# Token-major values, key blocks of 64 and two-turn attending in a six-layer local-attention kernel

## The chip, the cores and the metric

The kernel runs on one core of a Trainium2 chip. The metric is the device time of one execution in microseconds (us); less is better. TensorE is called PE here, ScalarE ACT, VectorE DVE, GpSimd POOL and the queue that issues the DMAs SP.

## The reference, cut to what matters

The input is 4 sequences of 512 tokens with 128 features. A global causal attention with 16 heads comes first; neither its code nor its work is changed. Then six layers follow, each a local attention and a gated feed-forward part. What the change touches is the local attention of every layer:

```
def attn_layer(x, Wqkv, qs, ksc, Wo):
    q, k, v = split(shift_tokens(x) @ Wqkv)          # 16 heads of 64 features
    q, k = rotary(l2norm(q) * qs), rotary(l2norm(k) * ksc)
    sim = einsum(q, k of this window of 32 and the one before) * 8
    sim = where(query < key or query > key + 32, -max, sim)
    return (softmax(sim) @ v) @ Wo
x = attn_layer(...) + x;  x = ffn_layer(shift_tokens(x), ...) + x
```

## The kernel before

The layers are a software pipeline written out by hand, one program for each engine, with a semaphore for each hand-over. A body is one layer of one sequence (24 bodies); it has two halves, `a = 0` and `a = 1`, each with 4 pairs of heads. There are 48 halves `n`. While half `n` is attended, the queries, keys and values of half `n + 1` are projected, and the feed-forward parts of earlier bodies are put in between (`v0`, `v1`, `v2`, `down`, `wo0`, `wo1` in a first half; `mean`, `var`, `g0`, `g1`, `g2` in a second one). PE's program for the middle 20 bodies is a loop of two bodies run 10 times; the other engines' programs are unrolled.

PE does the following in a half, in this order: `project` 0 and `value_tile` 0; `max_scores` in two parts, with `project` 1 and `value_tile` 1 around them; `norm2(0)`, `turn_max`; `project` 2; `turned_scores` for the even key windows, `value_tile` 2, `turned_scores` for the odd ones; `project` 3; `value_tile` 3; `norm2(1)`; `sum_probs`; `attend_local` for even windows, a feed-forward step, `attend_local` for odd windows.

- `project(i)` makes queries and keys of one pair of heads: each of the two is three passes of 512 columns over operands that POOL has split into a high and a low part (`three`, fp32r, one instruction each).
- `value_tile(t)` makes values of 128 tokens: 16 products of 32 tokens by 128 columns in plain fp32, put on the four column groups of PE, so that 32 keys of each pair lie on their own 32 partitions. A plain fp32 matmul shows as two in the trace, each with a weight load of its own.
- `turned_scores(e)` puts mask and row maximum into a bank with 2 bf16 products and adds 64 fp32 products of 32 keys by 64 queries; ACT takes the exponent of 1024 columns (`exps`).
- `sum_probs` sums over keys (8 products of 256 columns), ACT turns the sums to inverses by Ln and Exp (`invert_sums`, 256 columns), and SP stores and spreads them by DMA for POOL (`scale_out`).
- `attend_local(e)` adds 64 fp32 products of 32 keys by 64 queries.

One PSUM bank (`N_BANK`) serves the value tiles, the norms, the turned maxima and the sums in turn. `ring[0]` takes the projections, `ring[1]` and `ring[2]` the scores and what is attended. ACT empties banks in the order written in its own `body`: squares, `value_out`, `rnorm` (Ln and Exp of the norms), `max_rows`, `exps`, `invert_sums`. DVE rotates (`rope`) and multiplies by the spread norms (`final`), after which `max_scores` may start.

Of the kernel before, what the change touches and what calls it, by code (L numbers as in the profile page):

```python
# [7 lines left out]
F32 = mybir.dt.float32  # L8
# [26 lines left out]
BLOCKS = TOK // WINDOW  # L35
# [37 lines left out]
def shape_constants():  # L73
# [9 lines left out]
    token = np.arange(TOK)[None, :]  # L83
    own = np.arange(WINDOW)[:, None]
    by_key = np.zeros((P, TOK))
    for e in range(2):
        ahead = (token - WINDOW * e) % (2 * WINDOW) - own
        by_key[WINDOW * e:WINDOW * (e + 1)] = np.where((ahead >= 0) & (ahead <= WINDOW) & (token >= WINDOW * e),
                                                       0.0, MASKED)
    pick = np.zeros((P, 2, 2, P))  # L90
    for e in range(2):
        for h in range(2):
            for k in range(WINDOW):
                pick[WINDOW * e + k, e, h, k::WINDOW] = 1.0
            for pair in range(GROUP):
                pick[MAX_ROWS + 4 * (pair // 2) + 2 * h + pair % 2, e, h, WINDOW * pair:WINDOW * (pair + 1)] = 1.0
# [9 lines left out]
    in_pair = (part[:, None] // SLOT == col // (SLOT // GROUP)).astype(np.float32)  # L106
    squares = np.concatenate([eye, mean, in_head, in_pair], 1)
# [24 lines left out]
def build_program(nc, x, w_kqv, m, w_qkv, q_scale, k_scale, w_o, ln_g, ln_b, w_1, b_1, w_2, b_2,  # L132
                  rotary, masks, blocks, wide, out):
    with ExitStack() as ctx:
# [3 lines left out]
        def sem(name):  # L138
# [6 lines left out]
        MASKS = 2 * P + P + TOK + 4 * P  # L145
# [3 lines left out]
        warm16 = key_rows = mask_sb[:, 3 * P:3 * P + TOK]  # L149
        pick = [[mask_sb[0:MAX_ROWS + 8, 3 * P + TOK + (2 * e + h) * P:3 * P + TOK + (2 * e + h + 1) * P]  # L150
                 for h in range(2)] for e in range(2)]
        SQUARES = 2 * P + 2 * SLOT
        wide_sb = sb("wide_sb", [P, SQUARES + 2 * TOK + 12])
        eye, mean_w = (wide_sb[:, i * P:(i + 1) * P] for i in range(2))
        in_head, in_pair = (wide_sb[:, 2 * P + i * SLOT:2 * P + (i + 1) * SLOT] for i in range(2))
# [17 lines left out]
        w_hi = sb("w_hi", [P, 2, PAIRS, P], F32R)  # L173
        w_lo = sb("w_lo", [P, 2, PAIRS, P], F32R)
        wv_sb = sb("wv_sb", [P, PAIRS, P])
        w_raw = sb("w_raw", [P, 2, 2, P])
# [7 lines left out]
        x_shift = x_flat[:, 0:2 * TOK].rearrange("p (a t) -> p a t", a=2)  # L184
# [3 lines left out]
        raw = [sin_raw[:], x_flat[:, 2 * TOK:4 * TOK].rearrange("p (a t) -> p a t", a=2)]  # L188
# [198 lines left out]
        def queries(j, e):  # L387
            return min(2 * WINDOW, TOK - WINDOW * j)
# [5 lines left out]
        def _(sp):  # L394
# [68 lines left out]
            def store_inverses(n, a):  # L463
                sp.wait_ge(s_inv, n + 1)
                if some(n - 1):
                    sp.wait_ge(s_ib, 32 * (n - 1))
# [1181 lines left out]
```

## Time and profile before

| what | value |
|---|---|
| median of 3 runs | 2734.62 us (2728.51 to 2758.71) |
| profiled execution | 2722.72 us, its span 2720.9 us, 1.8 us around it |
| granted PE clock, mean | 0.872 |
| PE busy | 2033.8 us (75%), 44592 matmuls |
| PE weight loads busy | 1186.3 us (44%) |
| DVE, ACT, POOL busy | 1122.1, 1022.6, 949.9 us |
| chain that ended last | PE 61%, issue 14%, DVE 13%, ACT 8% |

### The profile page before, as it was taken

How to read it: one execution, taken by the hardware profiler on the slowest of the kernel's cores; microseconds unless marked ns; L12 is line 12 of the kernel's file. 1: busy time of each engine (PE TensorE's matmuls, PEld its weight loads, DVE VectorE, ACT ScalarE, POOL GpSimd, SP SyncE). 2: the span in 40 equal slices, each digit the busy share in tenths (PEclk: the TensorE clock that was granted, in tenths of full speed). 3: DMA queues.
4: the chain of work that ended last, by engine and by line, in shares of the span. 5: the costliest groups of instructions: out<-in, count | busy, mean ns of one | idle time of the engine just before them, and what ended most of it. 6: DMA issues, size and time to landing. Idle time of an engine off the chain costs nothing.

```text
span 2720.9 us, 96484 instructions
## 1 busy us (share of the span) xinstructions
PE 2033.8 (75%) x44592; PEld 1186.3 (44%) x44592; DVE 1122.1 (41%) x1198; ACT 1022.6 (38%) x1377; POOL 949.9 (35%) x621
## 2 busy tenths in 40 slices
PE   2999956777776777777778777777767777777875
PEld 1444434444444444444444444444444444444542
DVE  3444523354444434443433434344344344444441
ACT  1444423343333334333333433343333343344332
POOL 4222213233532434433344433235324244333320
PEclk9887768889898988899788799799889888899997
DMA  3000024454544544445445345444445444444441
GB/s 106 2 2 1 2 77 119 118 145 116 137 126 123 145 117 127 123 118 131 131 111 137 103 127 133 123 121 133 112 127 146 106 125 128 122 120 130 122 105 47
DMA packets 134834, 295.44 MB, mean 109 GB/s; under 512 B 23060, under 2 KB 48018, under 8 KB 127250
## 3 DMA queue, kind: packets, MB, share of 16 engines
q1 hardware_dynamic: 134418, 289.00, 39.6%
q8 instruction: 369, 6.05, 1.0%
q14 instruction: 47, 0.39, 0.0%
HBM read 177.54 MB, written 4.46 MB: 67 GB/s over the span
## 4 chain that ended last, share of the span: by engine, by line
PE 61%; issue 14%; DVE 13%; ACT 8%; DMA 1%; POOL 1%; SPq 1%; ACTq 0%; DVEq 0%; POOLq 0%
PE bank L996 6%; PE ring L979 5%; PE ring L694 5%; PE ring L952 5%; PE bank L901 4%; PE ring L696 4%; DVE rot L1507 4%; PE bank L877 4%; PE ring L695 4%; DVE rot L1500 3%; ACT sq L1218 3%; PE bank L1027 3%; ACT r_norm L1224 2%; PE bank L798 2%; PE ring L912 2%
## 5 line engine op out<-in xcount | busy, mean ns | idle before, releaser
L598 POOL TENSOR_TENSOR rot<-rot,t_sin 128x1024 f32<-128x1024 f32 x192 | 461.8, 2405 | 1306.8 <-DMA t_sin<-sin_raw 1306.8
L1496 DVE TENSOR_TENSOR sin_raw<-ring,tab_sb 128x1024 f32<-128x1024 f32 x192 | 235.1, 1225 | 1055.4 <-ACT sq L1218 995.7
L1218 ACT ACTIVATE sq<-ring 128x1024 f32<-128x1024 f32 x192 | 196.7, 1025 | 622.5 <-PE ring L696 622.5
L901 PE MATMUL bank<-wv_sb,x_tok 128*32 128x128 f32 x6144 | 236.9, 293 | 41.8 <-issue 41.6
L605 POOL TENSOR_TENSOR o_feat<-o_feat,inv_all 128x1024 f32<-128x1024 f32 x96 | 226.1, 2377 | 33.5 <-DMA inv_all<-inv_rows 33.5
L694 PE MATMUL ring<-xs_parts,w_hi 128*128 128x512 f32 x384 | 201.1, 524 | 45.3 <-issue 28.9
L1500 DVE TENSOR_TENSOR rot<-ring,tab_sb 128x1024 f32<-128x1024 f32 x192 | 233.2, 1215 | 0.0
L1507 DVE SCALAR_TENSOR_TENSOR rot<-r_all,rot 128x2048 f32<-128x2048 f32 x96 | 219.2, 2283 | 28.1 <-DMA r_all<-r_rows 27.8
L901 PEld LDWEIGHTS bank<-wv_sb,x_tok 128*32 128x32 f32 x6144 | 170.8, 116 | 123.0 <-issue 116.4
L1233 ACT ACTIVATE v_sb<-bank 128x512 f32<-128x512 f32 x192 | 114.8, 598 | 287.3 <-PE bank L901 287.1
L696 PE MATMUL ring<-xs_parts,w_lo 128*128 128x512 f32 x384 | 182.4, 475 | 44.3 <-issue 44.2
L979 PE MATMUL ring<-probs,v_sb 32*64 32x64 f32 (+1 forms) x12288 | 169.5, 236 | 54.0 <-issue 54.0
L979 PEld LDWEIGHTS ring<-probs,v_sb 32*64 32x64 f32 x12288 | 152.3, 135 | 104.6 <-issue 103.9
L1290 ACT ACTIVATE o_feat<-ring 128x1024 f32<-128x1024 f32 x96 | 97.9, 1022 | 217.5 <-PE ring L979 217.5
L695 PE MATMUL ring<-xs_parts,w_hi 128*128 128x512 f32 x384 | 179.3, 467 | 0.0
L996 PE MATMUL bank<-o_feat,wo_sb 128*128 128x512 f32 x384 | 174.9, 598 | 0.9 <-DVE state L1558 0.9
L952 PE MATMUL ring<-rot 64*32 64x64 f32 (+1 forms) x12288 | 153.2, 224 | 28.2 <-issue 27.8
L912 PE MATMUL ring<-mask_sb 128*128 128x512 bf16 x192 | 78.5, 501 | 126.3 <-DVE rot L1507 126.3
L952 PEld LDWEIGHTS ring<-rot 64*32 64x32 f32 x12288 | 133.7, 105 | 77.5 <-issue 77.4
L1430 DVE TENSOR_REDUCE inv_all<-ring 128x2 f32<-128x256 f32 (+3 forms) x128 | 104.0, 823 | 149.0 <-PE ring L758 148.3
L877 PE MATMUL bank<-sq,wide_sb 128*32 128x512 f32 x768 | 110.4, 646 | 49.5 <-ACT v_sb L1233 49.5
L694 PE MATMUL bank<-y_parts,w_hi 128*128 128x512 f32 x144 | 78.3, 543 | 87.3 <-DVE gates L1551 46.6
(147 smaller groups left out, 2918.2 us busy)
## 6 DMA issues: line engine op xcount, KB each, us to landing
t_sin<-sin_raw SPq DMA_DIRECT2D x384, 256.0 KB
r_all<-r_rows SPq DMA_DIRECT2D x192, 512.0 KB
inv_all<-inv_rows SPq DMA_DIRECT2D x96, 512.0 KB, 6.4
tab_sb<-in_rotary SPq DMA_DIRECT2D x6, 1024.0 KB
w_raw<-in_L_ffn_Wqkv SPq DMA_DIRECT2D x48, 128.0 KB, 3.4
wv_sb<-in_L_ffn_Wqkv SPq DMA_DIRECT2D x12, 256.0 KB, 6.7
wo_sb<-in_L_ffn_Wo SPq DMA_DIRECT2D x6, 512.0 KB, 8.9
x_tok<-state SPq DMA_DIRECT2D x24, 128.0 KB, 6.5
```

Of the source, the lines that this page charges most:

```text
L598: pool.tensor_tensor(dst, dst, t_sin[:], ALU.add).then_inc(s_rot, 1)
L694: pe.matmul(dst, lh, rh, start=True, stop=False)
L695: pe.matmul(dst, lh, rl, start=False, stop=False)
L696: return pe.matmul(dst, ll, rh, start=False, stop=True)
L901: mm = pe.matmul(N_BANK[SLOT * pair:SLOT * (pair + 1), j * P:(j + 1) * P], x_shift[:, par, at:at + WINDOW], wv_sb[:, 4 * a + pair, :], sta ...
L952: mm = pe.matmul(dst[SLOT * pair:SLOT * (pair + 1), h, at:at + wide_], rot[rows, a, pair, 1, at:at + WINDOW], rot[rows, a, pair, 0, at:at ...
L979: mm = pe.matmul(bank[2 + pair][DIM_HEAD * h:DIM_HEAD * (h + 1), at:at + wide_], v_sb[keys, a, col:col + DIM_HEAD], probs[keys, e, h, at:a ...
L996: mm = pe.matmul(F_BANK[:], wo_sb[:, a, :], o_feat[:, a, :], start=(a == 0), stop=(a == PAIRS - 1), skip_group_check=True)
L1218: act.activation(sq[:, i % 2, :, :], ring[0][:], ACT.Square).then_inc(s_sq, 1)
L1496: dve.tensor_tensor(sin_raw[:].rearrange("p a t -> p (a t)"), both, tab_sb[:, at + 2 * TOK:at + 4 * TOK], ALU.mult).then_inc(s_sin, 1)
L1500: dve.tensor_tensor(rot[:, a, i, :, :].rearrange("p a t -> p (a t)"), both, tab_sb[:, at:at + 2 * TOK], ALU.mult).then_inc(s_cos, 1)
L1507: dve.scalar_tensor_tensor(out=dst, in0=r_all[:], scalar=NORM_CAP, in1=dst, op0=ALU.min, op1=ALU.mult).then_inc(s_fin, 1)
```

## The change

Work is regrouped in the local attention of every layer; every result stays the same.

1. Values: `value_tile` is now `three` with the tokens as stationary operand: 3 fp32r passes of 512 columns in place of 32 matmuls. So the value weights have to be split too: `w_raw` loads three parts of a pair, and POOL's `split_pair` has 6 operations instead of 4. `wv_sb` and its loads go.
2. Keys lie in blocks of 64 with 96 queries each (4 strips of two blocks). `turned_scores(u)` makes all keys of two pairs of heads instead of half the keys of four. It uses `ring[1]` and `ring[2]` in both turns, so the second turn waits for both exponents of the first.
3. `sum_probs(u)` and `invert_sums(u)` run once for each turn, with 512 columns.
4. `attend_local(turn)`: 32 products of 64 keys by 96 queries each turn. The second turn adds to what the first wrote; PE waits for its own semaphore `s_at` between them.
5. `max_rows` is three copies instead of one. `x_shift` has one buffer instead of two.
6. SP stores inverses twice in a half.

```
-                for j in range(4):
-                    for pair in range(GROUP):
-                        at = WINDOW * (4 * t + j)
-                        mm = pe.matmul(N_BANK[SLOT * pair:SLOT * (pair + 1), j * P:(j + 1) * P],
-                                       x_shift[:, par, at:at + WINDOW], wv_sb[:, 4 * a + pair, :], start=True, stop=True)
-                mm.then_inc(s_v, 1)
+                rows = slice(t * P, (t + 1) * P)
+                three(N_BANK[:], (xs_parts[:, 2 * par, rows], xs_parts[:, 2 * par + 1, rows]),
+                      (w_hi[:, 2, 4 * a:4 * a + 4, :], w_lo[:, 2, 4 * a:4 * a + 4, :])).then_inc(s_v, 1)
...
+                    if some(n):
+                        pe.wait_ge(s_lns, 2 * n - 1)
...
+            def turned_scores(n, a, u):
+                if u == 0:
                     pe.wait_ge(s_nm, n + 1)
+                else:
+                    pe.wait_ge(s_e, 4 * n + 2)
+                for pair in range(2):
+                    dst = ring[1 + pair]
+                    for h in range(2):
+                        pe.matmul(dst[:, h, 0:STRIPS * SPAN], pick[4 * u + 2 * h + pair], key_rows[0:MAX_END, :],
+                                  start=True, stop=False, skip_group_check=True)
+                    for k in range(STRIPS):
+                        for c in range(2):
+                            at = KEYS * (2 * k + c)
+                            wide_ = queries(2 * k + c)
+                            for h in range(2):
+                                rows = slice(DIM_HEAD * h, DIM_HEAD * (h + 1))
+                                mm = pe.matmul(dst[KEYS * c:KEYS * (c + 1), h, SPAN * k:SPAN * k + wide_],
+                                               rot[rows, a, 2 * u + pair, 1, at:at + KEYS],
+                                               rot[rows, a, 2 * u + pair, 0, at:at + wide_],
+                                               start=False, stop=(k == STRIPS - 1), skip_group_check=True)
+                    mm.then_inc(s_st, 1)
...
+                strips = probs[:, u, :, :].rearrange("p i (k s) -> p i k s", s=SPAN)
+                for i in range(GROUP):
+                    dst = N_BANK[SLOT * i:SLOT * (i + 1), :].rearrange("p (k s) -> p k s", s=P)
+                    pe.matmul(dst[:, :, 0:SPAN], in_low, strips[:, i, :, :], start=True, stop=False,
+                              skip_group_check=True)
...
+            def attend_local(n, a, turn):
+                for u in range(2):
+                    for k in range(STRIPS):
+                        for c in range(2):
+                            pair = c if turn == 0 else 1 - c
...
@@ PE's body
                     turned_scores(n, a, 1)
+                    sum_probs(n, 0, end)
                     if not end:
                         project(gn, an, parn, 3)
...
-                    sum_probs(n, end)
+                    sum_probs(n, 1, end)
@@ ACT
+            def exps(n, u):
+                for pair in range(2):
+                    act.wait_ge(s_st, 4 * n + 2 * u + pair + 1)
...
+                    act.activation(probs[:, u, 2 * pair:2 * pair + 2, :], ring[1 + pair][:, :, 0:STRIPS * SPAN], ACT.Exp
+                                   ).then_inc(s_e, 1)
...
                     exps(n, 1)
+                    invert_sums(n, 0)
                     if a == 1:
                         mine.get("g0", nothing)()
                     if not end:
                         value_out(n + 1, 1 - a, 3)
                         rnorm(2 * n + 3)
-                    invert_sums(n)
+                    invert_sums(n, 1)
@@ SP's body
+                        if i == 3:
+                            store_inverses(n, a, 0)
                         if nxt:
                             swap_halves(4 * n + 4 + i)
```

PE in a second half, from the second scores to `project` 3, before: L945 is the mask product, L952 the scores, L694 to L696 the three passes.

```order
L945 MATMUL ring<-mask_sb 128x512 x2
L952 MATMUL ring<-rot 32x64 x56
L952 MATMUL ring<-rot 32x32 x8
...
L694 MATMUL ring<-xs_parts,w_hi 128x512
L695 MATMUL ring<-xs_parts,w_hi 128x512
L696 MATMUL ring<-xs_parts,w_lo 128x512
```

The same place now: L934 mask, L942 scores, L964 to L972 the first sums, L680 to L682 the three passes.

```order
L934 MATMUL ring<-mask_sb 128x384 x2
L942 MATMUL ring<-rot 64x96 x14
L942 MATMUL ring<-rot 64x64 x2
...
L964 MATMUL bank<-probs,wide_sb 32x4x96 x4
L968 MATMUL bank<-probs,wide_sb 32x4x64 x4
L972 MATMUL bank<-probs,wide_sb 32x3x32 x4
L680 MATMUL ring<-xs_parts,w_hi 128x512
```

The mask and the 16 products after it now come twice in a turn, and the first sums stand ahead of `project` 3.

ACT in a second half, before: the exponents (L1246), the value tile out (L1233), the squares (L1218), the exponents, the feed-forward gate (L1273), the last value tile out, the norms (L1224, L1227), the inverses (L1252, L1254).

```order
L1246 ACTIVATE probs<-ring 128x1024
L1233 ACTIVATE v_sb<-bank 128x512
L1218 ACTIVATE sq<-ring 128x1024
L1246 ACTIVATE probs<-ring 128x1024
L1273 ACTIVATE gates<-bank,b_sb 128x512
L1233 ACTIVATE v_sb<-bank 128x512
L1224 ACTIVATE r_norm<-bank,wide_sb 128x512
L1227 ACTIVATE r_norm<-r_norm,wide_sb 128x512
L1252 ACTIVATE inv_sums<-bank 128x256
L1254 ACTIVATE inv_sums<-inv_sums 128x256
```

ACT in a second half now: exponents L1264, value tile out L1246, squares L1231, first inverses L1271 and L1273, gate L1292, norms L1237 and L1240.

```order
L1264 ACTIVATE probs<-ring 128x768 x2
L1246 ACTIVATE v_sb<-bank 128x512
L1231 ACTIVATE sq<-ring 128x1024
L1264 ACTIVATE probs<-ring 128x768 x2
L1271 ACTIVATE x_tok<-bank 128x512
L1273 ACTIVATE x_tok<-x_tok 128x512
L1292 ACTIVATE gates<-bank,b_sb 128x512
L1246 ACTIVATE v_sb<-bank 128x512
L1237 ACTIVATE x_tok<-bank,wide_sb 128x512
L1240 ACTIVATE x_tok<-x_tok,wide_sb 128x512
```

The first inverses stand between the second exponents and the last value tile's exit; `value_tile` 3 on PE waits for their Ln.

## Rows read from the trace of the kernel before

**Rows 1.** Page, DMA queues and costliest groups: the instruction queue and the output projection.

```profile
q8 instruction: 369, 6.05, 1.0%
...
L996 PE MATMUL bank<-o_feat,wo_sb 128*128 128x512 f32 x384 | 174.9, 598 | 0.9 <-DVE state L1558 0.9
```

**Rows 2.** Windows: a first half, a second half, and the sum of four halves.

```profile
2127.71:2176.40 48.69, 40.27 (x866) 22.84 (x867) 20.62 (x21) 15.89 (x21) 16.54 (x9) 0.89 0.44 117
2176.40:2221.38 44.98, 30.81 (x850) 19.72 (x851) 18.44 (x16) 20.41 (x27) 17.92 (x9) 0.91 0.43 120
...
sum 190.52, PE 143.93 PEld 85.58 DVE 82.06 ACT 72.91 POOL 80.28; mean PE 35.98 PEld 21.40 DVE 20.52 ACT 18.23 POOL 20.07
```

**Rows 3.** Waits of PE: us in total, times, longest.

```profile
PE ring L912 <- DVE rot L1507: 126.3, 47, 11.8
PE ring L979 <- issue: 54.0, 33, 5.0
...
PE ring L923 <- issue: 44.2, 16, 5.3
PE ring L696 <- issue: 44.2, 19, 4.4
PE bank L901 <- issue: 41.6, 32, 2.3
...
PE ring L694 <- issue: 28.9, 9, 5.0
PE ring L952 <- issue: 27.8, 36, 3.7
```

**Rows 4.** Timeline of PE in a second half: start, length, what, [idle before].

```profile
2188.77 0.50 PE L694 MATMUL ring<-xs_parts,w_hi 128*128 128x512 f32 x1
...
2190.28 0.61 PE L945 MATMUL ring<-mask_sb 72*128 72x512 bf16 x2
2190.81 1.48 PE L952 MATMUL ring<-rot 64*32 64x64 f32 x128
2192.22 1.08 PE L901 MATMUL bank<-wv_sb,x_tok 128*32 128x128 f32 x32
...
2194.70 1.47 PE L952 MATMUL ring<-rot 64*32 64x64 f32 x125 [0.63 <-issue]
...
2200.54 0.59 PE L696 MATMUL ring<-xs_parts,w_lo 128*128 128x512 f32 x1 [3.69 <-issue]
...
2205.59 1.06 PE L877 MATMUL bank<-sq,wide_sb 128*32 128x512 f32 x8 [1.06 <-ACT v_sb L1233]
2207.45 1.07 PE L966 MATMUL bank<-probs,wide_sb 128*32 128x256 f32 x16 [0.80 <-ACT r_norm L1224]
2208.46 1.70 PE L979 MATMUL ring<-probs,v_sb 32*64 32x64 f32 x128
```

**Rows 5.** Timeline of ACT in the same second half.

```profile
2189.18 0.59 ACT L1239 ACTIVATE mask_sb<-bank 8x512 bf16<-8x512 f32 x1
...
2192.64 1.01 ACT L1246 ACTIVATE probs<-ring 128x1024 f32<-128x1024 f32 x1
...
2202.44 1.02 ACT L1218 ACTIVATE sq<-ring 128x1024 f32<-128x1024 f32 x1 [8.31 <-PE ring L696]
...
2206.72 0.69 ACT L1224 ACTIVATE r_norm<-bank,wide_sb 128x512 f32<-128x512 f32 x1 [1.27 <-PE bank L877]
2207.43 0.72 ACT L1227 ACTIVATE r_norm<-r_norm,wide_sb 128x512 f32<-128x512 f32 x1
```

**Rows 6.** Timeline of PE at the loop's jump back.

```profile
2308.74 0.79 PE L694 MATMUL ring<-xs_parts,w_hi 128*128 128x512 f32 x1 [5.03 <-issue]
```

**Rows 7.** Windows around an idle time of PE; the third number from the end is the clock.

```profile
2133.00:2137.00 4.00, 1.72 (x97) 1.36 (x96) 3.93 (x4) 0.63 (x2) 0.00 (x0) 1.00 0.33 131
2138.20:2144.90 6.70, 5.91 (x20) 2.38 (x20) 0.80 (x2) 2.71 (x4) 6.18 (x3) 0.51 0.02 5
```

**Rows 8.** Groups of POOL: the splitting of one pair's weights.

```profile
L585 POOL TENSOR_TENSOR w_hi<-w_raw,wide_sb 128x128 fp32r<-128x128 f32 x96 | 46.7, 508 | 118.3 <-DMA w_raw<-in_L_ffn_Wqkv 118.3
```

More of the change, by code:

```diff
@@ L105, in shape_constants @@
     in_head = (part[:, None] // DIM_HEAD == col // (SLOT // 2)).astype(np.float32)
-    in_pair = (part[:, None] // SLOT == col // (SLOT // GROUP)).astype(np.float32)
-    squares = np.concatenate([eye, mean, in_head, in_pair], 1)
+    in_part = [np.repeat(part[:, None] // KEYS == c, SLOT, 1).astype(np.float32) for c in range(2)]
+    squares = np.concatenate([eye, mean, in_head] + in_part, 1)
     row = np.arange(P) % SLOT
@@ L183, in build_program @@
         x_flat = x_tok[:].rearrange("p c d -> p (c d)")
-        x_shift = x_flat[:, 0:2 * TOK].rearrange("p (a t) -> p a t", a=2)
+        x_shift, r_norm, inv_sums, x_mid = (x_flat[:, i * TOK:(i + 1) * TOK] for i in range(4))
         v_sb = sb("v_sb", [P, 2, GROUP * TOK])
@@ L957, in sum_probs @@
-            def sum_probs(n, last):
-                pe.wait_ge(s_e, 2 * n + 2)
-                if not last:
-                    pe.wait_ge(s_ln, 2 * n + 4)
-                else:
-                    pe.wait_ge(s_nm, n + 1)
-                for e in range(2):
-                    for t in range(4):
-                        q = (t % 2) * TOK // 2
-                        mm = pe.matmul(N_BANK[SLOT * t:SLOT * (t + 1), 0:TOK // 2], in_pair,
-                                       probs[:, e, t // 2, q:q + TOK // 2], start=(e == 0), stop=(e == 1))
-                mm.then_inc(s_sm, 1)
@@ new lines, in attend_local @@
+            def attend_local(n, a, turn):
+                for u in range(2):
+                    for k in range(STRIPS):
+                        for c in range(2):
+                            pair = c if turn == 0 else 1 - c
+                            at, wide_ = KEYS * (2 * k + c), queries(2 * k + c)
+                            keys = slice(KEYS * c, KEYS * (c + 1))
+                            for h in range(2):
+                                col = TOK * k + P * (2 * u + pair) + DIM_HEAD * h
+                                mm = pe.matmul(ring[1 + u][DIM_HEAD * h:DIM_HEAD * (h + 1), pair, at:at + wide_],
+                                               v_sb[keys, a, col:col + DIM_HEAD],
+                                               probs[keys, u, 2 * pair + h, SPAN * k:SPAN * k + wide_],
+                                               start=(turn == 0 and k == 0), stop=(turn == 1 and k == STRIPS - 1),
+                                               skip_group_check=True)
+                mm.then_inc(s_at if turn == 0 else s_o, 1)
@@ L995, in run @@
                         for a in range(4 * half, 4 * half + 4):
+                            if a == PAIRS - 1 and not (isinstance(f, int) and f == BODIES - 1):
+                                pe.wait_ge(s_at, 2 * f + 3)
                             mm = pe.matmul(F_BANK[:], wo_sb[:, a, :], o_feat[:, a, :], start=(a == 0),
@@ L1018, in run @@
                             pe.wait_ge(f_he, 2 * NF * f + i)
+                        if i == 1 and not (isinstance(f, int) and f == BODIES - 1):
+                            pe.wait_ge(s_at, 2 * f + 4)
                         three(F_BANK[0:n, :], (w1_hi[:, off:off + n], w1_lo[:, off:off + n]), (y_hi, y_lo)
@@ L1088, in body @@
                         mine.get("g1", nothing)()
+                    if not new:
+                        pe.wait_ge(s_at, n + 1)
                     attend_local(n, a, 1)
```

229 lines of the change are left out of this document (103 added, 126 removed).

## Prediction

> **What bounds the kernel now.** I read the windows of single halves first, then PE's waits, then the timelines of PE and ACT in one half. A half takes 44.98 to 48.69 us, and PE is busy for 30.81 and 40.27 of them [rows 2]; no other engine comes near that. So PE sets the pace, and the question is what its idle time is. Two kinds count. One is a fixed hand-over between halves: PE waits for DVE's `final` at L912, 126.3 us in 47 halves [rows 3], since attended banks, squares, rotation and norms follow each other there. The other kind is "issue": 54.0 + 44.2 + 44.2 + 41.6 + 28.9 + 27.8 = 240.7 us [rows 3] in which no semaphore is missing. The timeline shows what that is. One such stall ends at 2194.70 and the next at 2200.54; between them stand 125 matmuls of L952 and one each of L694 and L695, 127 in all, which with their weight loads are 254 instructions [rows 4]. The instruction queue moved 6.05 MB in 369 packets, 16.4 KB each [rows 1]. So PE runs dry at the end of a block of some 256 instructions until the next has come. Short matmuls empty a block fastest: 127 of them are gone in about 1.5 us [rows 4].
>
> The Trainium skill, "Runtime: NRT & Kernel Launch", section Instruction fetch mechanics, says that instructions come in 16 KiB blocks of 256 and that crossing a block is mostly hidden. The block agrees with the trace, the hiding doesn't.
>
> **What the change takes off the instruction stream.** In the trace's matmuls a half has 858 (the loop's four halves have 3432 in the built program, 2088 now). Values go from 128 to 12, scores and masks from 260 to 136, sums from 16 to 48, attending from 256 to 128: 522 remain. At 127 a block that is 6.8 blocks a half before and 4.1 now. With as many stalls per block as now, 240.7 would become 146, a gain of 94. I take more, since a dense block now lasts longer: 127 matmuls of the new scores take about 2.9 us instead of 1.5, and those are the blocks that stall. The stall at the loop's jump back, 5.03 us [rows 6], I leave as it is: ten of them, 50 us. Of the other 190 I keep 60. Gain 130, with bounds of 94 and 190.
>
> **What PE's work costs, at full clock.** A pass of 512 columns takes 0.25 us (six from 2188.77 to 2190.28 [rows 4]); a value tile becomes 0.7 instead of 1.08, less 0.3 to 0.4. Before, 64 score matmuls of 64 columns fill 1.48 us, 11.6 ns per instruction [rows 4]; with 64 by 64 tiles only four run side by side instead of eight. For the rate of four side by side I take the value tile: 32 instructions of 128 columns in 1.0, 32 ns each, so 24 ns for 96 columns and 0.77 us for 32; the ends are the 11.6 ns of an unhindered instruction and 48 ns if only two tiles overlap. A group of two masks of 384 columns (0.4, from 0.53 for two of 512) and its 32 instructions is 1.15; a turn has two, 2.2 against 1.95 (2190.28 to 2192.22 [rows 4]). Attending: 64 instructions in 1.4 against 1.62 (L979 less its tail [rows 4]). Sums: one turn streams 384 + 256 + 96 = 736 columns per group of partitions where both parities together streamed 512 in 1.0 [rows 4], so 1.4 us, twice.
>
> **Second halves (`a = 1`).** In PE's order, per half:
> - The value tile ahead of the turned maxima: less 0.3. `max_rows` takes 0.59 [rows 5]; as three copies of 384, 256 and 96 columns about 1.2. `project` 2 hides 1.5 us of it: +0.2.
> - The second scores wait for both exponents of the first turn. ACT reaches them at 2192.64 as before [rows 5]; two of 768 columns at 0.8 end at 2194.3, so PE starts at 2194.5 instead of 2193.2: +1.2. The value tile lies inside that wait and saves nothing. Both turns of scores: +0.25.
> - The first sums are in series before `project` 3: +1.4.
> - From the end of `project` 3 to `norm2(1)` it is ACT that counts: 0.2 + squares 1.02, exponents 1.6, Ln 0.69, Exp 0.72, gate 0.7, value tile out 0.6, 0.15 = 5.7 us. Before, from the squares at 2202.44 to L877 at 2205.59 it was 3.15, with the 0.2 ahead 3.35 [rows 4, 5]. +2.3. PE has the gate's product (0.75) and a value tile (0.7) to do in it, and idles 4 us.
> - Second sums +0.4, two times attending -0.45.
> Sum: -0.3 + 0.2 + 1.2 + 0.25 + 1.4 + 2.3 + 0.4 - 0.45 = +5.0.
>
> **First halves (`a = 0`).** `down` hides the exponents. The chain of 5.7 has no gate in it, so 5.0, but the value tile may not start before its Ln at 3.7 and has its exit behind the Exp: `norm2(1)` at 5.3. Before, `wo0` (L996's 174.9 us over 48 calls of `wo0` or `wo1` are 3.6 us each [rows 1]), the value tile and 0.8 of wait made 5.4: no change. What is left: two value tiles -0.6, `max_rows` +0.2, scores +0.25, first sums +1.4, second +0.4, attending -0.45 = +1.2.
>
> A pair of halves is +6.2 at full clock; 24 bodies: **+149 us**.
>
> **Moved and added steps elsewhere.** SP now waits for the first inverses before it may issue the swap of `rope` 3; that swap, POOL's `add` and SP's norms behind it come about 2.3 us later. In second halves `norm2(1)` is itself 2.3 later, and in first halves the swap is needed only by the next half's `final`, which by the terms above starts over 10 us after `project` 3; so in ordinary halves I cost it at nothing. At the five changes of layer POOL does that `add`, one split and the next shifted input in a row, and `project` 0 waits for the last; the split is longer by two operations of some 0.4 (mean 508 ns [rows 8]). I take 3 us each, 15 in all. In the setup eight pairs are split one after another, +5. One buffer for `x_shift` costs nothing: POOL reads it at once and PE no longer reads it at all.
>
> **The clock.** After the window 2133 to 2137, in which PE was idle for 2.3 of 4 us, the granted clock went from 1.00 to 0.51 for the 6.7 us that follow [rows 7]; that is from 2.4 to 1.2 GHz, and matmuls of 512 columns take nearly twice as long. The new wait of 4 us in second halves does the same, I think in three of four; what follows (`norm2`, sums, attending) then costs 3.4 more: 24 x 0.75 x 3.4 = 60. Stalls that go give back some 35. Net +25, bounds 0 and +60.
>
> **Sum.** 149 - 130 + 15 + 5 + 25 = +64 on 2722.7, that is 2787; the median of the runs is 12 above the profiled one, so **2797 us**, 2.3% slower. With the best ends (stalls -190, clock 0, layer changes 0) it is 149 - 190 + 5 = -36; if scores and attending also come out 20% under my estimate, another -45: 2655. With the worst (-94, clock +60, and 15 more) it is +150: 2885.
>
> **Rivals.**
> - *The instruction supply was worth more than its gaps.* With 4.1 blocks a half nearly every stall but the jump back goes, and with them the half-speed stretches behind those of 3 us and more, which I price at another 50: 149 - 190 + 20 - 50 = -71, 2664 us. For it: the stalls of 3 us and more, like the one of 3.69 [rows 4], stand in second halves. Against: the long ACT chain stands there too. It decides once stalls and clock together give back over 170. Chance 0.29.
> - *The two cancel*: supply 165, clock +10: 149 - 165 + 20 + 10 = +14, within 1%. Chance 0.21.
> - *Tiles of 64 by 64 run only two at a time.* Then a score or attending matmul of 96 columns costs 48 ns instead of 24: 256 x 24 ns = 6.1 us a half, 48 halves: +290, about 3090. Against it: the value tile's and the norms' groups of four do overlap [rows 4]. Chance 0.03.
> - *Blocks are hidden, the issue gaps have another cause and stay.* By the page on the runtime that is the expectation; then 64 + 130 = +194, 2930 us. The spacing of 127 speaks against it. Chance 0.03.
> - *A floor per matmul.* If each small matmul cost 25 ns from start to start, 512 of them before and 256 now would save 6.4 us a half, 300 us, 2430 us. The trace has 128 in 1.48 us, 11.6 ns [rows 4], so 0.01. The Trainium skill, "TensorE: Matmul & The Clock Gate", section on 56 ns against 53.3 ns, gives that floor; the row is under half of it.
>
> **Chances.** The forecast itself has 0.43. Slower by over 1%: 0.43 + 0.03 + 0.03, and a little of the cancelling case, 0.50; within 1% 0.20; faster by over 1% 0.30. About 1% is what a measurement of this kernel can tell from no change, as its three runs spread by 1.1%. The range 2655 to 2885 takes in the forecast with its bounds, the cancelling case and the first rival. The likeliest case alone has 2760 to 2850.
>
> **What will show it.** In the new profile: some 16,000 fewer matmuls (48 x 336); "issue" before PE's lines near 110 us instead of 240.7; PE idle before the last value tile (by Ln of the inverses) about 3 us in second halves and near 0 in first ones; idle before the second scores about 1.2 us in second halves; a score group of 32 in 0.7 to 0.8 us; sums near 1.4; second halves at 49 to 52 us and first ones at 45 to 47. The forecast fails if the stalls fall under 60 us, or if the ACT chain after `project` 3 is shorter than 5 us.

## The result, and the profile after

The changed kernel takes 2753.11 us (median of 20 runs, 2731.11 to 2774.65), the kernel before 2733.3 us (20 runs, 2705.9 to 2758.71): a ratio of 1.0084, 95% interval 1.0056 to 1.0112. So it is slower by 0.8%, where 2.3% was forecast; the time lies in the range. Ratios here and below are of medians over the runs within 1.5% of their kernel's fastest; in the round of four experiments marked (A) only 4 of the 17 runs of the kernel before are such (median 2711.0 us, all 17: 2740.7; in the other rounds 2729 to 2746), so those four ratios may be up to 1% too high.

The page after, first lines and the instruction queue:

```profile
span 2728.8 us, 64800 instructions
## 1 busy us (share of the span) xinstructions
PE 2087.9 (77%) x28436; PEld 1175.4 (43%) x28464; DVE 1179.7 (43%) x1198; ACT 1164.3 (43%) x1665; POOL 997.5 (37%) x717
...
q8 instruction: 247, 4.05, 0.7%
```

247 packets of instructions answer to 369 [rows 1]. PE's waits after (us in total, times, longest):

```profile
PE ring L898 <- DVE rot L1527: 162.1, 48, 10.6
PE ring L680 <- issue: 55.6, 9, 7.3
PE bank L680 <- DVE gates L1571: 52.7, 26, 2.7
PE bank L680 <- ACT x_tok L1271: 49.8, 24, 3.0
PE bank L922 <- DVE neg_max L1534: 42.8, 25, 2.0
```

Set beside [rows 3], one entry carries most of the gain: issue falls from 240.7 us at six lines to 55.6 at one, the first matmul behind the jump back, nine times. Two are new or nearly so: the fourth value tile waits for the logarithm of the first sums (L1271), and the turning of the maxima waits for DVE's second reduction (L922; before 5.9 us in 5 places). The hand-over between halves (L898, before L912) grew from 126.3 to 162.1. Almost all of that growth stands at the start of second halves, where it was 66.9 us in all and is 99.9.

The same trade in one line each: 44 halves in the layers, before and then after (window, its us, busy us and count of PE, PEld, DVE, ACT, POOL, granted clock, DMA share, GB/s).

```profile
501.26:2593.08 2091.82, 1575.48 (x37740) 940.36 (x37740) 876.32 (x788) 799.46 (x1033) 786.40 (x490) 0.89 0.47 125
```

```profile
497.91:2598.97 2101.06, 1635.61 (x22956) 933.20 (x22957) 934.06 (x788) 928.94 (x1297) 828.95 (x571) 0.88 0.46 124
```

PE does 14,784 matmuls fewer and is busy for 60.1 us more; its idle time falls from 516.3 to 465.5. Fewer instructions aren't less work: the sums alone stream 1472 columns a half, per group of partitions, where they streamed 512. And it isn't second halves that grew, as was forecast, but first ones: on average 48.4 us (47.4 before) against 47.1 in second halves (47.7 before).

A second half after, the timeline of PE:

```profile
2179.77 0.39 PE L922 MATMUL bank<-mask_sb,neg_max 128*8 128x128 bf16 x4 [1.76 <-DVE neg_max L1534]
...
2187.86 0.50 PE L934 MATMUL ring<-mask_sb 104*128 104x384 bf16 x2
2188.29 0.88 PE L942 MATMUL ring<-rot 64*64 64x96 f32 x32
2189.10 0.85 PE L964 MATMUL bank<-probs,wide_sb 128*32 128x384 f32 x8
2189.76 0.61 PE L968 MATMUL bank<-probs,wide_sb 128*32 128x256 f32 x8
2190.20 0.35 PE L972 MATMUL bank<-probs,wide_sb 128*32 128x96 f32 x8
2190.47 0.50 PE L680 MATMUL ring<-xs_parts,w_hi 128*128 128x512 f32 x1
...
2195.14 0.79 PE L680 MATMUL bank<-w_hi,xs_parts 128*128 128x512 f32 x1 [2.28 <-ACT x_tok L1271]
...
2197.56 1.94 PE L863 MATMUL bank<-sq,wide_sb 128*32 128x512 f32 x8 [0.78 <-ACT v_sb L1246]
```

No block boundary stalls any more. The first sums stand in series, 2189.10 to 2190.47. The wait that ends at 2195.14 is the forecast one, shorter than forecast: 2.28 us. From the squares on ACT has no gap in this stretch, which is why PE waits:

```profile
2192.16 1.02 ACT L1231 ACTIVATE sq<-ring 128x1024 f32<-128x1024 f32 x1 [4.96 <-PE ring L682]
2193.09 1.51 ACT L1264 ACTIVATE probs<-ring 128x768 f32<-128x768 f32 x2
2194.47 0.62 ACT L1271 ACTIVATE x_tok<-bank 128x512 f32<-128x512 f32 x1
```

And the clock went down behind it, from 0.95 to 0.50 (1.2 GHz), as in [rows 7]:

```profile
2192.80:2195.10 2.30, 0.06 (x1) 0.00 (x0) 1.88 (x2) 2.28 (x4) 0.00 (x0) 0.95 0.00 0
2195.20:2202.90 7.70, 6.12 (x35) 1.98 (x35) 2.58 (x2) 3.13 (x5) 2.35 (x1) 0.50 0.19 73
```

### The profile page after: what moved, and what is told of

The parts are those of the page before. It is cut to its first block, busy times and chain, and to the rows that moved or that the text cites. A ratio compares the mean times of both kernels' runs of the same rounds, so it can differ in the third digit from the quotient of the medians.

```text
span 2728.8 us, 64800 instructions
## 1 busy us (share of the span) xinstructions
PE 2087.9 (77%) x28436; PEld 1175.4 (43%) x28464; DVE 1179.7 (43%) x1198; ACT 1164.3 (43%) x1665; POOL 997.5 (37%) x717
## 4 chain that ended last, share of the span: by engine, by line
PE 55%; DVE 15%; ACT 11%; issue 11%; DMA 3%; POOL 3%; SPq 2%; ACTq 0%; POOLq 0%; DVEq 0%
PE ring L680 5%; PE bank L1004 5%; PE ring L942 5%; DVE rot L1520 4%; PE ring L985 4%; DVE rot L1527 4%; PE ring L682 4%; PE ring L681 4%; ACT sq L1231 3%; DVE neg_max L1534 3%; PE bank L863 3%; PE bank L964 3%; ACT probs L1264 3%; PE ring L934 2%; PE bank L1037 2%
## 5 line engine op out<-in xcount | busy, mean ns | idle before, releaser
L1231 ACT ACTIVATE sq<-ring 128x1024 f32<-128x1024 f32 x192 | 196.8, 1025 | 670.8 <-PE ring L682 670.8
L680 PE MATMUL ring<-xs_parts,w_hi 128*128 128x512 f32 x384 | 203.5, 530 | 76.0 <-issue 55.6
L898 PE MATMUL ring<-mask_sb 128*128 128x512 bf16 x192 | 87.8, 554 | 162.1 <-DVE rot L1527 162.1
L682 PE MATMUL ring<-xs_parts,w_lo 128*128 128x512 f32 x384 | 183.2, 477 | 0.0
L681 PE MATMUL ring<-xs_parts,w_hi 128*128 128x512 f32 x384 | 182.8, 476 | 0.0
L942 PE MATMUL ring<-rot 64*64 64x96 f32 (+1 forms) x6144 | 174.8, 251 | 0.0
L1246 ACT ACTIVATE v_sb<-bank 128x512 f32<-128x512 f32 x192 | 114.6, 597 | 140.6 <-PE bank L682 140.1
L942 PEld LDWEIGHTS ring<-rot 64*64 64x64 f32 x6144 | 140.3, 137 | 65.3 <-issue 65.3
L1264 ACT ACTIVATE probs<-ring 128x768 f32<-128x768 f32 x192 | 148.7, 809 | 23.2 <-PE ring L942 23.2
L985 PE MATMUL ring<-probs,v_sb 64*64 64x96 f32 (+1 forms) x6144 | 157.9, 253 | 0.2
L985 PEld LDWEIGHTS ring<-probs,v_sb 64*64 64x64 f32 x6144 | 139.8, 141 | 35.5 <-issue 30.3
L680 PE MATMUL bank<-y_parts,w_hi 128*128 128x512 f32 x144 | 74.6, 518 | 105.0 <-DVE gates L1571 52.7
L863 PE MATMUL bank<-sq,wide_sb 128*32 128x512 f32 x768 | 119.6, 697 | 42.0 <-ACT v_sb L1246 42.0
L1237 ACT ACTIVATE x_tok<-bank,wide_sb 128x512 f32<-128x512 f32 x96 | 66.0, 687 | 189.2 <-PE bank L863 189.2
```

What stands on the lines that cost most here:

```text
L680: pe.matmul(dst, lh, rh, start=True, stop=False)
L681: pe.matmul(dst, lh, rl, start=False, stop=False)
L682: return pe.matmul(dst, ll, rh, start=False, stop=True)
L942: mm = pe.matmul(dst[KEYS * c:KEYS * (c + 1), h, SPAN * k:SPAN * k + wide_], rot[rows, a, 2 * u + pair, 1, at:at + KEYS], rot[rows, a, 2 * ...
L985: mm = pe.matmul(ring[1 + u][DIM_HEAD * h:DIM_HEAD * (h + 1), pair, at:at + wide_], v_sb[keys, a, col:col + DIM_HEAD], probs[keys, u, 2 * ...
L1231: act.activation(sq[:, i % 2, :, :], ring[0][:], ACT.Square).then_inc(s_sq, 1)
```

## The experiments

All ratios are to the kernel before, with 95% intervals. "Changed" is the changed kernel, at 1.0084. The profiles are of single runs, so a difference of a few us between two of them says little.

### The values alone

```diff
-for j in range(4): for pair in range(GROUP): pe.matmul(N_BANK[...], x_shift[...], wv_sb[...])
+three(N_BANK[:], (xs_parts hi, lo at rows), (w_hi[:, 0, 4 * a:4 * a + 4, :], w_lo[...]))
```

> The kernel before with the value part of the change alone: the 16 small products of a value tile are replaced by three passes of 512 columns over the split input and split weights. The weights used are those of the queries, so the values, and the output with them, are not the reference's; the amount of work is that of the changed kernel. Theory (the gain is the instruction supply): the value products lose their issue stalls (L901 41.6 us) and shares of their neighbours' (L923 44.2, L952 27.8, L979 54.0), since some 29 of 32 instructions of each tile are gone; TensorE's issue stalls in the layers fall from 235.7 us to between 150 and 205, and the tile's work by 0.3 us a half, 14 us; the time falls by 40 to 95 us, to 0.965 to 0.985 of the kernel before. Rival (stalls are set by where the stream is densest, in scores and attending, which stay as they are): the stalls stay above 215 us, and the time falls by the tile's 14 us and no more, to 0.990 to 0.998.

Measured: 0.9745 (0.9637 to 0.9854) (A). The values come out wrong, since the queries' weights stand in for theirs; the amount of work is right. Waits of PE, issue first, then two others:

```profile
PE bank L696 <- issue: 47.7, 11, 6.4
...
PE ring L979 <- issue: 27.6, 20, 3.4
PE ring L696 <- issue: 26.8, 10, 4.6
...
PE ring L952 <- issue: 10.2, 25, 1.7
```

```profile
PE ring L912 <- DVE rot L1507: 161.7, 48, 10.7
...
PE bank L936 <- DVE neg_max L1514: 47.8, 26, 2.0
```

112 us of issue stalls are left of 240.7. The theory holds, and its size was again too small: I expected 150 to 205. The value part by itself is a gain of 2.5%, so the rest of the change costs 3.4 points, some 90 us; with the interval and the base of this round it can be anything from 60 to 150. The other two rows matter as much: the longer hand-over (161.7) and the wait for the maxima (47.8) of the changed kernel are here too, without key blocks of 64, second sums or a longer chain on ACT. So they come with the values' part; that they are waits which the stalls had hidden is the likely reading. One-pass values come out with 128 tokens on the partitions, and the changed kernel's attending follows that layout; whether blocks of 32 keys could have been kept with it was not tried.

### The sums cut short

```diff
-# per head: 384 + 256 + 96 columns, accumulated, in each turn
+# per head: 384 + 128 columns in the first turn, 32 in the second
```

> The changed kernel with the sums cut to about the columns of the kernel before: 512 a head group in the first turn and 32 in the second, in place of 736 and 736 (before: 512 in all). Part of each sum is left out, and most of the second, so the attended values aren't scaled rightly. Theory (between the run with the values alone, 0.975, and the changed kernel, 1.008, stand some 90 us, and they are the sums' longer work in series: 1.6 us a half more than before): the time falls by 60 to 90 us, to 0.975 to 0.987. Rival (the sums' work is partly hidden, by ScalarE's exponents and gates that TensorE then waits for, and the blocks of 64 in scores and attending cost the rest): the time falls by less than 40 us, above 0.994.

Measured: 0.9851 (0.9786 to 0.9917), so 64 us less than changed: the theory holds at its lower end. The sums are about two thirds of those 90 us, if 90 is right; what the rest is no run shows. By the timeline's means over all halves it is the second turn's cut that shows: from the second norms to the end of attending 8.4 us a half instead of 9.5. From the turned maxima to the end of the last projection, where the first turn stands, a half takes 12.6 us, as in changed (12.5); why the 0.5 us cut there doesn't show I can't say.

### The first sums late

```diff
 turned_scores(n, a, 1)
-sum_probs(n, 0, end)
 project(gn, an, parn, 3) ... value_tile(gn, an, parn, 3); norm2(n + 1, 1)
-sum_probs(n, 1, end)
+sum_probs(n, 0, end)
 attend_local(n, a, 0)
+sum_probs(n, 1, end)
```

(ACT's `invert_sums(n, 0)` goes behind `rnorm(2n + 3)`, SP's `store_inverses(n, a, 0)` ahead of the second, and the waits go with them.)

> The changed kernel with its first sums of exponents moved on TensorE from ahead of the last projection of a half to behind the second norms, and their inversion on ScalarE behind those norms. Theory: the 49.8 us in 24 places that TensorE waits for the logarithm of the first sums ahead of the fourth value tile go away, and the stretch from the last projection to the second norms is back at 3.4 us in second halves (4.9 us in the changed kernel), which is worth 36 us; the second sums then wait for the logarithm of the first, which costs at most 0.5 us a half, 24 us. The time falls by 20 to 55 us, to 0.988 to 1.001 of the kernel before. Rival (the sums only move behind the norms and are late there just as much, 1.4 us in series): the ratio stays at 1.004 to 1.012, with 1.4 us more between the norms and the end of attending.

Measured: 1.0598 (1.05 to 1.0695) (A). Both theories fell. The wait for L1271's counterpart did go (49.8 to 5.9 us), but ACT's waits have an entry that I had not thought of:

```profile
ACT x_tok L1264 <- DMA inv_rows<-x_tok: 329.0, 48, 8.1
```

The second logarithm writes the buffer from which SP stores the first inverses, and that store now stood in SP's queue behind the second norms' trip through memory. Behind ACT's wait stood the gate for which PE waits, 131 us instead of 41.4:

```profile
PE bank L679 <- ACT gates L1285: 131.3, 48, 5.8
```

The remedy was a second buffer:

```diff
-act.wait_ge(s_id, 16 * (2 * n + u)); act.activation(inv_sums, N_BANK[:], ACT.Ln)
+act.wait_ge(s_id[u], 16 * n);        act.activation(inv_two[u], N_BANK[:], ACT.Ln)
```

> The kernel with the late first sums (0.6 to 1.0 here, at 1.060) with a second buffer for the inverted sums and a semaphore of its own for each buffer's store, nothing else. Theory (formed from that run: ScalarE waited 293 us in 42 places until the first inverses were stored, because the second logarithm writes the same buffer, and the gates behind it on ScalarE held TensorE): these waits go, TensorE's waits for gates fall from 131 to some 50 us, and what the late sums were meant to give shows: 0.985 to 1.003 of the kernel before. Rival (the late place itself costs, since the sums stand in series behind the norms and the hand-over to the next half is late): the store's wait goes, but the ratio stays above 1.015.

Measured: 0.9965 (0.9928 to 1.0002). The theory holds: ACT no longer waits for the store, PE's wait for the gates is back at 41.2 us, and the late place is worth 1.2% against changed. So the early place cost something, but with one buffer it was the better one. The sums stand in series in either place: from the second norms to the end of attending it is 10.6 us a half here and 9.5 in changed.

### VectorE's first maxima early

```diff
-if not end: rope(gn, an, 1)
 maxima(n, 0)
+if not end: rope(gn, an, 1)
```

> The changed kernel with one move: VectorE takes the first maxima of a half ahead of the rotation of the next half's second pair, where the changed kernel takes them behind it. Theory (the change traded instruction-supply stalls for new waits): in the changed kernel TensorE waits 42.8 us in 25 places for the second maxima at its turning step; these go down to under 10 us, the second pair's rotation comes 1.3 us later but its swap has slack, and the time falls by 15 to 40 us, to 0.994 to 1.003 of the kernel before (the changed kernel is at 1.008). Rival (the wait only hides another, since VectorE is late as a whole there): the wait goes to the next gather of the same half, for the rotated keys of the second pair or for the norms, and the ratio stays at 1.005 to 1.012.

> The kernel before with VectorE's first maxima of a half taken ahead of the rotation of the next half's second pair: the move that took the changed kernel from 1.008 to 0.986. Theory (the wait for the maxima came with the change, because the change made TensorE's stretch up to there shorter by some 2 us; before, its own issue stalls hid it, with 5.9 us of waits for the maxima in 5 places): nothing to win here, 0.995 to 1.004. Rival (VectorE's order is bad in both kernels, and the change has nothing to do with it): 0.975 to 0.988, as in the changed kernel.

Measured: 0.9862 (0.9767 to 0.9957) for changed with the move (A), 0.9868 (0.9817 to 0.992) for the kernel before with it. PE's waits in changed with the move:

```profile
PE bank L680 <- DVE gates L1571: 30.6, 26, 2.6
...
PE bank L922 <- DVE neg_max L1534: 9.0, 10, 0.9
```

The first run gave more than its theory's range, and the second contradicts its theory: most of the gain isn't the change's. What the two share is the wait for `gates` (52.7 to 30.6 here; 46.6 to 19.6 in the kernel before): the gated products queue on DVE behind the maxima, and came earlier with them. The wait at L922, 42.8 to 9.0, is what changed has more of, and could answer to its larger gain, 2.2% against 1.3%; but the intervals of the two gains overlap, so that isn't shown.

### TensorE's loop written out

```diff
-with pe.Fori(0, BODIES // 2 - 2) as i:
-    body(2 * i + 2, 0)
-    body(2 * i + 3, 1)
+for g in range(2, BODIES - 2):
+    body(g, g % 2)
```

> The changed kernel with TensorE's loop over bodies written out in full, so that nothing jumps back; the other engines are as they were. Theory: the only issue stalls left in the changed kernel, 55.6 us in 9 places, all stand at the jump back and are the fetch of instructions from an address that isn't the next one; they go, and the time falls by 35 to 55 us, to 0.988 to 0.996 of the kernel before. Rival (a straight program fetches the same blocks, and the stalls turn up at other places, or the wait is hidden in the wait of others behind it): issue stalls of over 30 us remain somewhere, and the ratio is 1.002 to 1.012.

> The kernel before with TensorE's loop over bodies written out. Theory (two kinds of fetch: one at the jump back, 5.0 us each time in 9 places, and one at every 256th instruction wherever the stream is dense): the first kind goes, 30 to 50 us, the other 190 us of issue stalls stay; 0.980 to 0.990. Rival (the loop is what makes the fetch late everywhere, since a straight program can be read ahead): most of the 236 us go, and the ratio is below 0.96. Other rival (straight code is no cheaper): 0.995 to 1.005.

Measured: 0.993 (0.9868 to 0.9993) for changed (A), 0.9873 (0.9824 to 0.9923) for the kernel before. In changed, issue falls from 55.6 to 2.5 us. In the kernel before, the stalls at the jump are gone and the others have grown, as its waits show:

```profile
PE ring L979 <- issue: 95.4, 49, 5.2
PE ring L952 <- issue: 70.6, 48, 5.3
PE bank L901 <- issue: 51.2, 32, 4.1
```

That is 217 us, where the same kernel with its loop had 28.9 at the jump and 212 elsewhere. Both theories hold: there are two kinds of stall, one at the jump and one in dense code. In changed the jump costs 6.2 us each time (55.6 in nine), in the kernel before 3.2 at the jump itself.

### Both moves, on either kernel

> The changed kernel with both moves that gained by themselves: the first maxima early on VectorE (0.986 of the kernel before) and TensorE's loop written out (0.993, and 1.008 without). Theory: they take away different waits (VectorE's maxima ahead of the turning step; the fetch at the jump back) and add up: 0.965 to 0.977. Rival (one covers the other: the jump back stands just ahead of the first scores of a half, where TensorE waits for the rotated keys anyway): 0.980 to 0.988.

> The kernel before with both moves that the changed kernel got in the run at 0.950: the first maxima early on VectorE (alone 0.987) and TensorE's loop written out (alone 0.987). It is the fair partner of that run. Theory (the kernel before is held back by its instruction supply, so that stalls taken away at one place come back at another: with the loop written out alone 211 us of issue stalls were left of 236): the two add up at best, 0.970 to 0.982, with 180 to 215 us of issue stalls, so that the change is worth 2 to 3.5% once VectorE's order and the jump back no longer hide it. Rival (the change is worth nothing even there): 0.945 to 0.958.

Measured: 0.9502 (0.9447 to 0.9557) for changed with both moves, 0.9748 (0.9675 to 0.982) for the kernel before with both. The first is beyond its theory's range (0.965 to 0.977). That need not mean that the gains did more than add: the range was made from two ratios of round (A). The medians add up by themselves, 2753 us for changed, 2667 and 2685 with one move each and so 2599 for both, where 2604 was measured. The second holds to its theory, with 190 us of issue stalls left. The pair answers the question of what the change is worth where neither the jump nor DVE's order stands in its way: 0.9502 / 0.9748 = 0.975, that is 2.5% faster, with some 1% of uncertainty either way. 44 halves of each, changed first:

```profile
505.18:2475.86 1970.68, 1590.18 (x22956) 917.42 (x22957) 951.57 (x788) 926.55 (x1297) 833.66 (x570) 0.90 0.49 132
```

```profile
496.48:2528.11 2031.63, 1577.84 (x37740) 953.34 (x37740) 933.77 (x788) 802.46 (x1033) 795.77 (x491) 0.89 0.49 129
```

PE is busy for 12 us more and idle for 73 us less.

### The supply by itself

First the projections in pieces: the same columns, 168 more matmuls a half.

```diff
-pe.matmul(dst, lh, rh, ...)                       # 512 columns, three passes
+for k in range(8): pe.matmul(dst[:, cols], lh, rh[:, cols], ...)   # 64 columns each
```

> The changed kernel with each pass of the projections of queries and keys given to TensorE as eight matmuls of 64 columns in place of one of 512: the same columns and the same results, 168 instructions more a half (690 in place of 522; 858 before, 742 in the run with the values alone, which had 109 us of issue stalls). Theory (stalls are set by how many instructions TensorE takes per time): issue stalls away from the jump back appear, 30 to 120 us of them, and the projections' work grows little; 1.02 to 1.06. Rival (the stalls of before came from the dense runs of scores and attending alone): no issue stalls but the jump back's 56 us; the time grows only as far as the pieces themselves are slower, 1.005 to 1.02.

Measured: 1.4947 (1.4833 to 1.5062), issue 45.8 us, all at the jump. Neither theory holds: the stalls away from the jump didn't come, and the time grew by 49%. The run doesn't tell, since the pieces were far slower than the pass: a half took some 75 us, and so the rate of instructions fell, to 9 matmuls per us. Then short bf16 matmuls, added ahead of each projection's product:

```diff
+for j in range(21):   # 42 in the second run
+    pe.matmul(bank[k][SLOT * (j % 4):SLOT * (j % 4 + 1), 0:SLOT], eye16[:, 0:SLOT], eye16[:, 0:SLOT], ...)
 mm = three(bank[k][:], ...)
```

> The changed kernel with 21 short bf16 matmuls (32 columns onto 32 partitions, overwritten by what follows) ahead of each projection of one 512-column product: 168 a half, so 690 TensorE matmuls a half in place of 522 (858 before, 742 with the values alone). Theory (the count of instructions over time sets the stalls): issue stalls appear away from the jump back, between 5 and 60 us of them, less than the 60 us above the jump's share in the run with the values alone. Rival (the stalls of before were a matter of the many small fp32 products in a row, not of the count): none but the jump back's 50 us. The added matmuls' own time is some 12 to 30 ns each, 95 to 240 us in 48 halves, so the time itself decides nothing.

> The same with 42 ahead of each product: 336 a half, 858 TensorE matmuls, as many as in the kernel before. Theory: issue stalls of 120 to 260 us, as before's 236, and the half grows by 4 to 10 us of added matmuls besides. Rival: the jump back's 50 us alone, or below 80 us.

Measured: 1.0647 (1.0602 to 1.0691) and 1.1279 (1.1237 to 1.1322). Issue waits of the first, then of the second:

```profile
PE ring L854 <- issue: 43.0, 9, 5.0
...
PE ring L912 <- issue: 3.4, 5, 1.6
```

```profile
PE ring L854 <- issue: 98.2, 40, 3.8
...
PE ring L912 <- issue: 17.6, 15, 2.8
PE ring L682 <- issue: 3.4, 1, 3.4
PE ring L680 <- issue: 3.1, 1, 3.1
```

The issue stalls of the layers, against the rate of matmuls (their count a half by the mean time of a half). In three of these kernels a second stall stands close by the jump, in most of its nine occurrences: 22 matmuls ahead of it in the kernel before, 3 ahead with the values alone, 38 behind with 336 added. Whether these belong to the jump no run says, so they have a column of their own.

| kernel | matmuls a half | us a half | per us | at the jump, us | within 40 matmuls of it | elsewhere |
|---|---|---|---|---|---|---|
| changed | 522 | 47.8 | 10.9 | 55.6 | 0 | 0 |
| late sums, two buffers | 522 | 47.8 | 10.9 | 45.6 | 0 | 24 |
| 168 added | 690 | 50.9 | 13.6 | 43.0 | 0 | 3 |
| 336 added | 858 | 55.3 | 15.5 | 29.6 | 23 | 71 |
| values alone | 742 | 45.9 | 16.2 | 26.2 | 42 | 45 |
| before | 858 | 47.5 | 18.0 | 28.9 | 28 | 183 |

With 168 added the 3.4 us are below the 5 that the theory named as the least, so that run alone is nearer to its rival. With 336 added there are 122 us in all, just above the theory's least of 120, and the rival (below 80) fell. So short bf16 matmuls added to the changed kernel do bring stalls back, and small fp32 products are not needed for them. The kernel before and the one with 336 added have the same 858 matmuls a half, and so the same number of blocks, with 183 and 71 us of stalls elsewhere: the number of blocks doesn't set them. The mean rate doesn't set them alone either: the values alone have fewer than 336 added at a higher rate, and the late sums have 24 us at the rate at which changed has none, nearly all inside the first scores. How dense the stream is at one place may count too; no run separates the two.

### All moves

> The changed kernel with all moves: first maxima early, no loop on TensorE (these two: 0.950) and the late first sums with two buffers for the inverses (which took the changed kernel from 1.008 to 0.997). Theory: the late sums take away the wait for the first logarithm (39 us in the run at 0.950), and give back part of it behind the norms: 0.935 to 0.947. Rival (with the other waits gone the sums in series behind the norms weigh more): 0.948 to 0.960.

Measured: 0.9325 (0.9253 to 0.9398), 2538.74 us: faster than the kernel before by 6.8% and than changed by 7.5%, a little beyond its theory's range (0.935 to 0.947). The page:

```profile
span 2534.1 us, 64091 instructions
## 1 busy us (share of the span) xinstructions
PE 1992.2 (79%) x28436; PEld 1145.4 (45%) x28464; DVE 1193.1 (47%) x1198; ACT 1168.1 (46%) x1665; POOL 1001.6 (40%) x717
```

```profile
496.40:2405.97 1909.57, 1539.93 (x22956) 902.52 (x22957) 946.03 (x788) 932.61 (x1297) 832.72 (x571) 0.93 0.51 136
```

The same 22,956 matmuls take 96 us less of PE's time than in changed, at a granted clock of 0.93 for 0.88. Waits that go take half-speed stretches with them.

## Why the prediction was off

**What held.** PE sets the pace; the issue stalls are the supply of instructions, in blocks of 256; the change trades them for more columns and a longer chain on ACT. The count fell by the forecast 16,000. A turn of sums takes 1.37 us at full clock, two exponents 1.51, the logarithm 0.62, all near the terms.

**The step that failed is the size of the supply term.** I took 130 us (bounds 94 and 190); it gave 185. I kept 60 us of stalls besides the jump back, because I scaled stalls by the number of blocks and corrected by feeling. What the runs show in its place: none elsewhere than at the jump at 10.9 matmuls per us, 212 us at 18.0, and at the same number of blocks 94 or 212. The number of blocks alone doesn't set the stalls. Both signs that I had named for a failure came: the stalls fell under 60 us (55.6), and ACT's chain was shorter than 5 (4.9).

**Terms that were too large.** The second scores' wait for the first exponents, forecast at 1.2 us in each second half (29 us in all), is 7.1 us in 14 places in the whole trace: scores were as slow as ACT. 22 us less. From the end of `project` 3 to `norm2(1)` it took on average 4.9 us instead of 3.4 in second halves, so +1.5 where I had +2.3; 20 us less. At the changes of layer PE waited 3.9 us in five places where I had 15.

**A term that was too small.** I priced a turn of scores at 2.2 us against 1.95 and then put 0.25 down for both turns together. It takes 2.48 (2186.62 to 2189.10), so +0.53 twice a half: 51 us where my sum had 12. A group of 32 takes 0.88 where I had 0.77.

**Terms that were missing.** The wait for the maxima (+37 us) and the longer hand-over (+36 us), both also there with the values alone. I looked for what ACT would be late with, and at DVE not at all: its order (rotation, then maxima, 2.35 us for two) was hidden by the stalls of PE. A stall of 2.80 us stood just there in the half at 2176 of the kernel before.

The clock's +25 and the setup's +5 can't be read apart; the granted clock over 44 halves went from 0.89 to 0.88, with the forecast fall to 0.50 behind the wait of 2.28 us.

**Where the time went.** Over the 44 halves the profiled runs differ by 9.2 us: PE is busy for 60.1 more and idle for 50.9 less. The idle time is made up so: issue -168, the wait for the first logarithm +44, the maxima +37, the hand-over +33, the gates +15, the norms ahead of the turned maxima -17, the rest +5. The busy time I can't split as well: scores give +47 (44 halves at 1.06), and sums, attending, values and the clock share the rest. My terms corrected one by one don't add up to the 8 us between the profiled runs, or to the 20 between the medians: 64 - 55 - 22 - 20 - 11 + 39 + 37 + 36 is +68; some of the waits probably hide behind one another, which no run shows. That the measured time fell into the range is thus in part luck: a gain taken 55 us too small stood against 73 us of waits that I had not seen.

**The rivals.** The cancelling case came, with other parts than I gave it (supply 165, clock +10). "The supply was worth more than its gaps" had the right supply, 185 us, but the half-speed stretches didn't go with it (the clock fell from 0.89 to 0.88), and the two missing waits took the gain back. That block boundaries are hidden is true of the changed kernel away from its jump, with 0 us of stalls, and not of the kernel before, with 212. The Trainium skill, "Runtime: NRT & Kernel Launch", section Instruction fetch mechanics, calls the crossing mostly hidden, without naming a rate; the trace agrees for the changed kernel alone. Of the two on small tiles, "only two at a time" fell with 32 instructions of 96 columns in 0.88 us, 27 ns each and not 48. The floor of 25 ns fell with 2753 us where it gave 2430; the 27 ns say nothing against it.

## What to carry to other kernels

When many small instructions run an engine dry, don't scale the stalls by their number: look at instructions per us, on average and at the densest place, in kernels with and without stalls; and where they go, ask of every other engine what its order was hiding behind them. A step moved later on an engine needs its buffers moved too: one buffer, stored through a queue, turned a gain of 1.2% into a loss of 4 to 5%. And a change of small effect can be one of real effect behind somebody else's wait: tried together with two unrelated moves, this one was worth 2.5%.

## What the runs showed of the hardware

- PE's stalls for instructions away from a jump are more at a higher mean rate of matmuls, each with its weight load, but don't follow it alone: 0 and 24 us at 10.9 per us, 3 at 13.6, 71 at 15.5, 45 at 16.2, 183 at 18.0.
- At a loop's jump back PE stalls for 2.4 to 6.2 us (21.8 with the sums late and one buffer, 55.6 in changed, each in nine), in three kernels for 5.8 to 7.5 with what stands within 40 matmuls of it; straight code left 2.5 us in all in the changed kernel.
- Splitting an fp32r pass of 512 columns into eight of 64 made it about four times slower at full clock: 16 pieces start within 1.81 us (2005.21 to 2007.02), 113 ns each, so 0.9 us for 512 columns, where a pass of 512 takes 0.23 to 0.25. Each piece has a weight load of its own, and the loads follow each other without a gap, so they are the likely limit. Over the whole run, at a mean clock of about 0.7, it is 1663 us in 9216 matmuls, 180 ns each:

```profile
2005.21 1.98 PE L687 MATMUL ring<-xs_parts,w_hi 128*128 128x64 f32 x16
2007.02 1.07 PE L687 MATMUL ring<-xs_parts,w_lo 128*128 128x64 f32 x8
```

```profile
L687 PE MATMUL ring<-xs_parts,w_hi 128*128 128x64 f32 x6144 | 1050.6, 336 | 61.7 <-issue 45.8 <-POOL xs_parts L600 10.4 <-DVE rot L1527 4.4
L687 PE MATMUL ring<-xs_parts,w_lo 128*128 128x64 f32 x3072 | 612.4, 357 | 0.0
```

```profile
L687 PEld LDWEIGHTS ring<-xs_parts,w_hi 128*128 128x128 f32 x6144 | 1013.7, 257 | 92.1 <-issue 73.5
L687 PEld LDWEIGHTS ring<-xs_parts,w_lo 128*128 128x128 f32 x3072 | 582.5, 282 | 0.0
```
